# Sorted experts run inside the MLP's block, on two groups of batches, in the MLP's tiles

## The chip, the core and the metric

One core of one Trainium2 chip runs the whole program. The number is the device time of one execution in microseconds, the median of several; a second number is the span of the one execution that the hardware profiler recorded. The engines are PE (TensorE, matmuls and transposes), DVE (VectorE), ACT (ScalarE), POOL (GpSimd) and SP (SyncE, which here only issues DMAs). PEld is PE's weight load, which overlaps its matmuls.

## The reference, cut to what matters

Two layers run one after the other on x of 4 batches x 512 tokens x 256 channels. The first has attention and a 16-expert layer; the second has a gated convolution, an MLP and, last, a top-1 layer of two experts. The change touches only the end of the second layer:

```python
x = x + m                      # the MLP of the second layer, relu(h W_mlp1) W_mlp2, 256 -> 1024 -> 256
h = _layernorm(x) * (1 + cb) + sb
logits = h @ gate_w.T          # 2 experts
probs = softmax(logits)
sel = argmax(probs); top_w = probs[sel]
# each expert: 256 -> 1024 -> 256
y = (silu(h @ w_gate[e].T) * (h @ w_up[e].T)) @ w_down[e].T     # e = sel, for each token
x = x + gb * (top_w * y)       # the output
```

## The kernel before

All arithmetic is fp32, done as products of fp32r pieces: a value is split into a high part (an ACT copy to fp32r) and a low part (a DVE subtraction), and each product is two or three matmuls. B = 4 batches of T = 512 tokens, each TT = 4 tiles of 128 tokens, NT = 16 tiles in all.

**MLP and dispatch** (`mlp_and_dispatch`, one block of five engine programs). `interleave` is the order of every engine: for b in 0 to 5 and i in 0 to 7 it calls `tile(b, i)` (only while b < 4) and the stages written as (back, at, stage), each in turn (b, at) for batch b - back. Turn (b, i) is the name used below. On PE, `up` and `down` are the MLP's matmuls (printed as L49 to L51, the helper `split3`). A batch's dispatch lags its MLP: in turn (b+1, 3) PE transposes the MLP's result to rows (`rows`, L2238) and DVE adds it to X and takes layer-norm statistics (`residual`, L2118, L128); DVE centres and scales the rows (`center_rows` L2134, `scale_rows` L2141) with a root from POOL (L2035); in turn (b+1, 6) PE transposes them back (`columns`, L2247) and ACT and DVE split them into hT (L2072, L2148); in (b+2, 0) PE computes the gate's logits (`gate`, L2259, 16 small matmuls); DVE and ACT turn them into the expert choice and the share (`center`, `exponential` L2081, `choose`); in (b+2, 2) PE counts tokens ahead (`ranks`, L2267, L2268) and DVE writes each token's slot (`place`, L2186); POOL scatters the rows by four indirect DMAs (L2042) into `d_sorted`, expert 0's tokens from the front and expert 1's from the back, over 17 blocks of 128 slots. So turns (4, i) and (5, i) hold only dispatch: that of batch 2 and then the whole chain of batch 3. PS is the PSUM, eight banks: the MLP's tiles use 2 to 5, its result 6 and 7, the dispatch 0 and 1. The second layer's up weights (`up_hi`, `up_lo`) are loaded and split beside the MLP into `u_hi`, `u_lo`.

**Sorted experts** (`sorted_experts`, a block of its own, which begins when every engine has left the block before). SP waits for all scatters, loads blocks of slots into `x_xg` (L2346) and the down weights (L2340). The work is 17 blocks x 4 steps, each of 256 of the 1024 hidden channels. `steps` is the order on each engine: at step s PE does `columns` for the block that starts at s+2 (L2483), `up(s)` (12 matmuls of 512 columns, L2538 to L2540), `rows(s-1)` (two transposes of h, L2506) and `down(s-2)` (L2523 to L2526); ACT does `silu(s)` (L2400) and the high part of h (L2405); DVE does the product (`times`, L2446) and the low part (L2450). Up results alternate over three PSUM banks and transposed h over two. Every block's result goes out by one indirect DMA of POOL to `x_results` (L2375); after the last block all four batches' results are loaded (L2361), multiplied by gb (L2466), added to X (L2470) and stored (L2366). In the first four steps ACT and DVE also split the down weights into `x_w` (L2386, L2422).

Of the kernel before, what the change touches and what calls it, by code (L numbers as in the profile page):

```python
# [15 lines left out]
P = 128  # L16
# [19 lines left out]
L1_BLOCKS = NT + L1_EXPERTS - 1  # L36
# [1861 lines left out]
class Dispatch:  # L1898
# [5 lines left out]
    def __init__(self, k, c):  # L1904
# [3 lines left out]
        self.token, self.back, self.first = sb("token", [NT]), sb("back", [NT]), sb("first", [L1_BLOCKS])  # L1908
# [18 lines left out]
def mlp_and_dispatch(k, conv, H, hT, weights, gate_w, d, up_w, up_d):  # L1927
# [6 lines left out]
    with ExitStack() as c:  # L1934
# [18 lines left out]
        jump = k.sb(n("jump"), [P, TT], F32, c)  # L1953
        S = lambda s: k.sem(n(s))
# [36 lines left out]

        def up_tiles(j):
# [3 lines left out]
        def sync(sp):  # L1996
            def load_rows(b):
# [14 lines left out]
            for i in range(PARTS):  # L2012
# [8 lines left out]
        def gpsimd(pool):  # L2021
            pool.wait_ge(conv.z_ready, B * IT)
# [5 lines left out]
            pool.iota(d.back[:], pattern=[[-P, NT]], base=L1_BLOCKS * P - 1, channel_multiplier=-1,  # L2028
                      allow_small_or_imprecise_dtypes=True).then_inc(filled, 1)
            pool.iota(d.first[:], pattern=[[P, L1_BLOCKS]], base=0, channel_multiplier=0,  # L2030
# [13 lines left out]
            wavefront((0, root), (0, scatter))  # L2044
            yield

        def scalar(act):
            def split(i):
# [38 lines left out]
            yield from interleave(tile, (0, 0, up_part(0, up_hi)), (0, 4, up_part(1, up_hi)), (0, 6, up_part(2, up_hi)), (0, 7, result),  # L2087
                       (1, 0, gate), (1, 6, columns), (2, 1, exponential))

        def vector(dve):  # L2090
            own = Chain(dve, own_dve)
# [21 lines left out]
            def residual(b):  # L2113
# [8 lines left out]
                if b == 0:  # L2122
                    dve.wait_ge(g_hi, 1)
                    dve.tensor_tensor(g2[:, :, 1, :], gst[:], f32(g2[:, :, 0, :]), ALU.subtract).then_inc(g_lo, 1)
                    dve.wait_ge(filled, 4)
# [38 lines left out]
            def choose(b):  # L2164
# [8 lines left out]
                                       initial=d.count[:, b * TT - 1:b * TT] if b else 0.0, op0=ALU.add, op1=ALU.add).then_inc(n_ready, 1)  # L2173
# [5 lines left out]
                own.link(dve.tensor_tensor(jump[:], jump[:], d.token[:, cols], ALU.add))  # L2179
                own.wait()  # L2180

            def place(b):

                cols = slice(b * TT, (b + 1) * TT)
                dve.wait_ge(p_ready, b + 1)
                dve.tensor_tensor(d.slots[:, cols], jump[:], before, ALU.subtract).then_inc(slots_done, 1)  # L2186
                if b == B - 1:
                    dve.wait_ge(t_ready, 1)
                    own.link(dve.tensor_copy(d.n1[:], total))
                    own.wait()  # L2190
                    own.link(dve.tensor_scalar(d.slots_f[:, 0:L1_BLOCKS - 1], d.first[:, 0:L1_BLOCKS - 1], d.n1[:, 0:1], None, ALU.add))
                    own.wait()
                    dve.tensor_scalar(d.expert[:, 0:L1_BLOCKS - 1], d.slots_f[:, 0:L1_BLOCKS - 1], float(B * T), None, ALU.is_ge).then_inc(d.expert_ready, 1)
# [4 lines left out]
            yield from interleave(tile, (0, 1, up_part(0, up_lo)), (0, 5, up_part(1, up_lo)), (0, 7, up_part(2, up_lo)), (0, 7, add_h),  # L2198
                       (1, 3, residual), (1, 4, center_rows), (1, 5, scale_rows), (1, 6, columns_lo), (2, 0, center), (2, 1, choose), (2, 2, place))

        def tensor(pe):
            def up(b, i):
# [434 lines left out]
```

## Time and profile before

| | |
|---|---|
| median of 3 executions | 1180.3 us (1177.23 to 1182.08) |
| the profiled execution: its own time | 1183.18 us |
| its span in the trace | 1181.1 us |
| busy in the span: PE, DVE, ACT, POOL | 81%, 63%, 55%, 39% |
| last large matmul of the MLP begins | 960.92 us |
| last slot of batch 3 written | 981.93 us |
| first expert matmul, last expert matmul | 993.81 us, 1160.22 us |

Times in the trace count from the span's start. A row of a timeline is start, duration, engine, line and operation, and in brackets how long the engine had been idle and what ended that. A row of a table by stretch gives, for each engine, the busy time and the number of instructions, then the clock granted to TensorE (1.00 is 2.4 GHz, 0.50 is 1.2 GHz), then the share of the DMA engines and GB/s.

### The profile page before, as it was taken

What the parts mean: (1) busy time and instruction counts of PE and PEld (TensorE: products, weight loads), DVE (VectorE), ACT (ScalarE), POOL (GpSimd) and SP (SyncE); (2) the same over time, 40 slices, a digit from 0 to 9 for tenths busy, and PEclk for the clock granted to TensorE, in tenths of its full rate; (3) what the DMA queues carried; (4) which work ended last, traced back from release to release, by engine and by line L of the source; (5) the groups of instructions that cost most, each with busy time, mean ns of one, the idle gap of its engine ahead of it and who ended that gap; (6) DMA issues with size and microseconds to landing.
All of it is one profiled execution on the core that took longest, in us unless ns stands there. A gap on an engine that the chain in (4) does not pass through costs nothing. (4 is left out here: it accounts for less than half of the span.)

```text
span 1181.1 us, 21152 instructions
## 1 busy us (share of the span) xinstructions
PE 958.2 (81%) x5454; PEld 800.5 (68%) x5454; DVE 742.6 (63%) x1917; ACT 650.9 (55%) x1693; POOL 454.9 (39%) x637
## 2 busy tenths in 40 slices
PE   6678799999978743678999991479899974999993
PEld 2467688888866632557999990367687753888882
DVE  4875799999956653248655552898546773444444
ACT  3568889999952532248666662469744322333331
POOL 3477466666630665402444443475500221011000
PEclk9788999999988775789999996699899985999996
DMA  6067844444315222309444437410042203001104
GB/s 245 18 211 187 196 104 91 100 91 97 64 50 165 99 77 81 122 25 315 128 127 126 119 109 271 143 72 1 15 128 82 76 28 125 23 28 32 32 15 151
DMA packets 109546, 123.13 MB, mean 104 GB/s; under 512 B 44160, under 2 KB 82560, under 8 KB 109336
## 3 DMA queue, kind: packets, MB, share of 16 engines
q1 hardware_dynamic: 100856, 98.93, 29.4%
q0 software_dynamic: 8608, 23.20, 5.3%
q8 instruction: 40, 0.66, 0.2%
q14 instruction: 42, 0.34, 0.1%
HBM read 77.73 MB, written 44.35 MB: 103 GB/s over the span
## 5 line engine op out<-in xcount | busy, mean ns | idle before, releaser
L741 ACT ACTIVATE PR<-PS,nmax 128x128 f32<-128x128 f32 (+3 forms) x256 | 135.6, 552 | 12.8 <-DVE nmax L781 11.5
L658 POOL TENSOR_SCALAR PR<-PR,rinv 128x128 f32<-128x128 f32 (+3 forms) x256 | 131.9, 536 | 0.0
L781 DVE TENSOR_REDUCE nmax<-PS 128x1 f32<-128x128 f32 (+3 forms) x256 | 113.6, 481 | 19.9 <-PE PS L684 14.3
L1379 POOL DMA_INDIRECT r_results<-r_y,r_to x79 | 75.8, 960 | 113.5 <-DVE r_to L1434 77.3
L789 DVE TENSOR_TENSOR PTlo<-PS,PThi 128x512 fp32r<-128x512 f32 (+1 forms) x192 | 103.0, 590 | 2.9 <-ACT PThi L751 2.9
L751 ACT ACTIVATE PThi<-PS 128x512 fp32r<-128x512 f32 (+1 forms) x192 | 96.8, 545 | 5.7 <-PE PS L696 5.6
L683 PE MATMUL PS<-K,Q 128*128 128x128 f32 (+3 forms) x256 | 84.2, 388 | 10.9 <-DMA Q<-q_parts 6.7
L696 PE MATMUL PS<-ident,PR 128*128 128x128 f32 x640 | 85.8, 279 | 3.2 <-DVE PTlo L789 2.6
L712 PE MATMUL PS<-PThi,V 128*128 128x512 f32 (+3 forms) x256 | 85.3, 346 | 1.0 <-DVE PTlo L789 0.5
L2446 DVE TENSOR_TENSOR x_h<-PS,x_sg 128x256 f32<-128x256 f32 x68 | 28.9, 425 | 86.6 <-ACT x_sg L2400 86.6
L2400 ACT ACTIVATE x_sg<-PS 128x256 f32<-128x256 f32 x68 | 26.2, 385 | 96.0 <-PE PS L2540 96.0
L973 POOL DMA_INDIRECT r_sorted<-o_hrow,o_slots x64 | 64.2, 1004 | 38.5 <-issue 18.7
L2375 POOL DMA_INDIRECT x_results<-x_y,x_to x17 | 16.3, 961 | 157.0 <-DVE x_to L2441 144.6
L712 PE MATMUL PS<-PTlo,V 128*128 128x512 f32 (+3 forms) x256 | 76.2, 323 | 0.0
L1423 DVE TENSOR_TENSOR r_xlo<-PS,r_xhi 128x256 fp32r<-128x256 f32 x79 | 33.4, 423 | 65.8 <-issue 52.5
L696 PEld LDWEIGHTS PS<-ident,PR 128*128 128x128 f32 x640 | 68.7, 142 | 8.8 <-DVE PTlo L789 5.0
L2538 PE MATMUL PS<-r_wlo,r_xhi 128*128 x158 | 59.5, 376 | 2.8 <-issue 2.6
L1394 ACT ACTIVATE r_xhi<-PS 128x256 fp32r<-128x256 f32 x79 | 30.4, 385 | 56.1 <-PE PS L2540 52.7
L683 PEld LDWEIGHTS PS<-K,Q 128*128 128x128 f32 x256 | 51.2, 203 | 13.6 <-issue 6.4
L684 PE MATMUL PS<-maskb,identb 128*128 128x128 bf16 x256 | 60.4, 236 | 0.0
L2524 PE MATMUL PS<-x_w,x_hhi 128*128 (+1 forms) x136 | 57.2, 437 | 1.7 <-DVE x_hlo L2450 1.7
L741 ACT ACTIVATION_READ_ACCUMULATOR PR<-PS,nmax 128x1 f32 x256 | 58.4, 228 | 0.0
(378 smaller groups left out, 3079.6 us busy)
## 6 DMA issues: line engine op xcount, KB each, us to landing
r_xg<-r_sorted SPq DMA_DIRECT2D x79, 129.0 KB
r_wst<-in_routed SPq DMA_DIRECT2D x16, 608.0 KB
K<-k_parts SPq DMA_DIRECT2D x64, 128.0 KB
Q<-q_parts SPq DMA_DIRECT2D x32, 128.0 KB
Q<-q_parts SPq DMA_DIRECT2D x64, 64.0 KB
V<-v_parts SPq DMA_DIRECT2D x64, 64.0 KB, 2.4
mlp_st<-r_results SPq DMA_DIRECT2D x8, 512.0 KB, 7.2
c_yg<-r_results SPq DMA_DIRECT2D x8, 512.0 KB, 8.2
```

The source lines that it names most:

```text
L658: pool.tensor_scalar(PR[:, e % 4, i, 0:w], PR[:, e % 4, i, 0:w], rinv[:, e % 4, i:i + 1], 1.0, ALU.mult, ALU.mult).then_inc(norm_done, 1)
L683: pe.matmul(k.PS[:, i, 0:w], Q4[u][:, s // 2, P * i:P * i + P], K4[u][:, s, 0:w], start=True, stop=False)
L684: pe.matmul(k.PS[:, i, w - P:w], k.identb[:], k.maskb[:], start=False, stop=True).then_inc(s_ready, 1)
L696: ins = pe.transpose(k.PS[:, 4 + bank, at % 512:at % 512 + P], PR[:, (e - TRANS) % 4, i, P * j:P * j + P], k.ident[:])
L712: ins = pe.matmul(O[:, P * j:T], V4[u][:, j, s, :], pt[:, ge % 2, PT_AT[j]:PT_AT[j] + w], start=(s == 0 and j == 0 and part == 0), stop=(s ...
L741: act.activation(PR[:, e % 4, i, 0:w], k.PS[:, i, 0:w], ACT.Exp, bias=nmax[:, e % 4, i:i + 1], accum_out=rsum[:, e % 4, i:i + 1]).then_inc ...
L751: act.activation(PThi[:, e % 2, at:at + w], k.PS[:, 4 + n, 0:w], ACT.Copy).then_inc(hi_done, 1)
L781: dve.tensor_reduce(nmax[:, e % 4, i:i + 1], k.PS[:, i, 0:P * (i + 1)], AX_X, ALU.max, negate=True).then_inc(max_done, 1)
L789: dve.tensor_tensor(PTlo[:, (e - LO) % 2, at:at + w], k.PS[:, 4 + n, 0:w], f32(PThi[:, (e - LO) % 2, at:at + w]), ALU.subtract).then_inc(l ...
L973: pool.indirect_dma_start(out=d.sorted, out_offset=bass.IndirectOffsetOnAxis(ap=slots[:, b * TT + t, choice:choice + 1], axis=0), in_=hrow ...
L1379: pool.indirect_dma_start(out=d.results, out_offset=bass.IndirectOffsetOnAxis(ap=to[:, i % TO_LANES:i % TO_LANES + 1], axis=0), in_=y[:, i ...
L2538: pe.matmul(out, x_hi, w_lo, start=first, stop=False)
```

## The change

`sorted_experts` is no longer a block. It returns programs for each engine, which `interleave` of the renamed `mlp_dispatch_and_experts` advances by one step per turn while b is 4 or 5, ahead of that turn's dispatch stages, and which then run on alone. The tokens are sorted in two groups, batches 0 and 1, and batches 2 and 3, each with 9 blocks (8 + 1 for the boundary between the experts), so there are 18 blocks and 72 steps. A group's blocks need only its own two batches' scatters; the first group's results are loaded beside the second's blocks and added to X in steps 56 to 63; only the second group's follow the last block. The tiles come from those of the MLP: block rows, silu and product in `H`, the down weights in the first two batches of `hT` and in the MLP's weights, others in the MLP's staging. The down weights are split in turns (3, 5), (3, 6) and, the last two, on ACT in (4, 0), (4, 1) and on DVE in (4, 1), (4, 2). PSUM: up results alternate over two banks (before three), transposed h has one (before two).

```diff
+L1_GROUPS = 2
+GROUP_BATCHES = B // L1_GROUPS
+GROUP_BLOCKS = NT // L1_GROUPS + L1_EXPERTS - 1
+L1_BLOCKS = L1_GROUPS * GROUP_BLOCKS
...
-        def interleave(tile, *others):
+        def interleave(experts, tile, *others):
             for b in range(B + 2):
                 for i in range(MLP_T):
                     if b < B:
                         tile(b, i)
+                    else:
+                        next(experts)
                     for back, at, stage in others:
...
+            next(experts)
             load_rows(3)
-            yield
+            yield from experts
...
-            wavefront((0, root), (0, scatter))
+            def first_result(b):
+                if b == B - 1:
+                    next(experts)
+            wavefront((0, root), (0, first_result), (0, scatter))
+            yield from experts
...
-                       (1, 0, gate), (1, 6, columns), (2, 1, exponential))
+                       (1, 0, gate), (1, 6, columns), (2, 1, exponential), (0, 5, down_part(0, x.down_hi(act))), (0, 6, down_part(1, x.down_hi(act))),
+                       (1, 0, down_part(2, x.down_hi(act))), (1, 1, down_part(3, x.down_hi(act))))
...
-        UP, XT, HT, Y = (0, 1, 2), 3, (4, 5), (6, 7)
+    UP, XT, HT, Y = (2, 3), 4, 5, (6, 7)
...
-                wait(pe, h_done, s - 2)
+            wait(pe, h_done, s - 1)
...
-                wait(pe, hlo_done, s - 1)
+            wait(pe, hlo_done, s)
...
+        def load_down(i):
+            if i < 2:
+                sp.wait_ge(own_h, 2 * (i + 1))
+            else:
+                sp.wait_ge(w2_done, i - 1)
...
+        sp.wait_ge(own_h, 6)
+        for i in range(3):
+            load_block(i)
+        load_down(2)
+        load_down(3)
...
+        for i in range(3, N):
+            load_block(i)
+            if i == G + 3:
+                load_results(0)
+        store(0)
+        load_results(1)
+        store(1)
...
+        def first_group(s):
+            at = s - (G + 5) * C
+            if 0 <= at < 4 * GROUP_BATCHES:
+                (added if at % 2 else scaled_rows)(at // 4, at // 2 % 2)
```

How the order moves on PE, after the MLP's last matmul. Before, only dispatch stands there (L2259 gate, L2267 and L2268 ranks, L2238 rows, L2247 columns), then the change of block and the first block's columns (L2483):

```order
L2259 MATMUL PS<-m_g,hT 128x4 x16
L2267 MATMUL PS<-d_count,onesb 128x4
L2268 MATMUL PS<-d_second,later 128x4
L2238 MATMUL PS<-ident,mlp_st 128x128 x8
L2247 MATMUL PS<-ident,m_h 128x128 x8
L2259 MATMUL PS<-m_g,hT 128x4 x16
L2267 MATMUL PS<-d_count,onesb 128x4
L2268 MATMUL PS<-d_second,later 128x4
L2270 MATMUL PS<-d_count,onesb 128x1
L1934 UNCONDITIONAL_BRANCH
L2472 UNCONDITIONAL_BRANCH
L2483 MATMUL PS<-ident,x_xg 128x128 x2
```

Now, from the end of the second expert step's up matmuls in turn (4, 3) (L2629 to L2631 are up, L2583 rows of h, L2289 the dispatch's rows, L2559 columns of a block; `H` and the `m_` tiles are those of the MLP):

```order
L2629 MATMUL PS<-u_lo,m_hi 128x512
L2630 REGISTER_ALU
L2630 MATMUL PS<-u_hi,m_lo 128x512
L2631 MATMUL PS<-u_hi,m_hi 128x512
L2583 MATMUL PS<-ident,H 128x128 x2
L2289 MATMUL PS<-ident,mlp_st 128x128 x8
L2559 MATMUL PS<-ident,H 128x128 x2
L2629 ISA
L2629 MATMUL PS<-u_lo,m_hi 128x512
```

PE's rows for batch 3 now stand behind two expert steps and behind the transposes of h of the first, which wait for ACT and DVE.

On ACT, before, from the MLP's last result (L2062) to the first silu (L2400):

```order
L2062 ACTIVATE mlp_st<-PS,modc 128x512 x2
L2081 ACTIVATE m_ex<-m_lg 128x8
L2072 ACTIVATE hT<-PS 128x512 x2
L2081 ACTIVATE m_ex<-m_lg 128x8
L1934 UNCONDITIONAL_BRANCH
L2380 UNCONDITIONAL_BRANCH
L2395 ACTIVATE x_xhi<-PS 128x256
L2400 ACT_TABLE_LOAD
L2400 ACTIVATE x_sg<-PS 128x256
```

Now, on the same stretch (L2104 the MLP's result, L2467 the block's high part, L2611 the down weights, L2123 the exponential, L2472 silu):

```order
L2104 ACTIVATE mlp_st<-PS,modc 128x512 x2
L2467 ACTIVATE m_hi<-PS 128x256
L2611 ACTIVATE m_whi<-H 128x4x256
L2123 ACTIVATE m_ex<-m_lg 128x8
L2611 ACTIVATE m_wlo<-H 128x4x256
L2472 ACT_TABLE_LOAD
L2472 ACTIVATE H<-PS 128x256 x2
```

Two splits of down weights and a table load now stand between the MLP's last result and the first silu, and batch 3's exponential comes later, between silu(7) and silu(8).


On DVE, in turns (4, 2) to (4, 5), batch 3's residual, statistics, centring and scaling (L2162, L133 to L2165, L2178, L2185) alternate with the experts' product and low part (L2511, L2515):

```order
L2511 TENSOR_TENSOR H<-PS,H 128x256
L2234 TENSOR_TENSOR d_slots<-m_jump,PS 128x4
L2617 TENSOR_TENSOR m_wlo<-H,m_wlo 128x4x256
L2511 TENSOR_TENSOR H<-PS,H 128x256
L2515 TENSOR_TENSOR m_wlo<-PS,m_whi 128x256
L2162 TENSOR_TENSOR X<-PS,X 128x512 x2
L133 BN_STATS m_stats<-X 128x6 x4
L136 BN_AGGR m_mv<-m_stats 128x2 x4
L2165 TENSOR_SCALAR m_var<-m_mv 128x4
L2493 TENSOR_TENSOR m_lo<-PS,m_hi 128x256
L2511 TENSOR_TENSOR H<-PS,H 128x256
```

The third of these rows, a down-weight split, and the product of each step now stand ahead of batch 3's dispatch.

## Rows read from the trace of the kernel before

**Rows 1.** Table by stretch; the columns are explained above.

```profile
961.15:993.81 32.66, 10.92 (x57) 8.87 (x55) 12.21 (x53) 3.84 (x8) 9.02 (x10) 0.55 0.16 52
993.81:1160.62 166.81, 165.05 (x848) 134.75 (x848) 71.09 (x204) 61.29 (x173) 15.37 (x16) 0.98 0.12 39
1160.62:1181.10 20.48, 0.00 (x0) 0.00 (x0) 10.20 (x17) 0.47 (x1) 0.96 (x1) 0.55 0.61 211
1010.97:1143.96 132.99, 132.99 (x702) 109.67 (x700) 55.48 (x169) 47.43 (x140) 13.45 (x14) 1.00 0.08 27
```

**Rows 2.** Timeline: batch 1's last scatter, then from the MLP's end to the experts' start.

```profile
945.51 0.96 POOL L2042 DMA_INDIRECT d_sorted<-m_h,d_slots  x1 [0.30 <-issue]
...
961.15 1.84 PE L2259 MATMUL PS<-m_g,hT 128*128 128x4 f32 x16
...
961.35 1.27 ACT L2062 ACTIVATE mlp_st<-PS,modc 128x512 f32<-128x512 f32 x2 [3.48 <-PE PS L51]
...
986.25 0.96 POOL L2042 DMA_INDIRECT d_sorted<-m_h,d_slots  x1 [0.30 <-issue]
...
992.10 0.69 PE L2483 MATMUL PS<-ident,x_xg 128*128 128x128 f32 x2 [10.41 <-DMA x_xg<-d_sorted]
```

**Rows 3.** Timeline of one steady expert step, engines PE, ACT and DVE.

```profile
1140.71 0.38 PE L2506 MATMUL PS<-ident,x_h 128*128 128x128 f32 x2
...
1141.67 0.41 DVE L2450 TENSOR_TENSOR x_hlo<-PS,x_hhi 128x256 fp32r<-128x256 f32 x1
...
1143.03 0.38 PE L2506 MATMUL PS<-ident,x_h 128*128 128x128 f32 x2
```

**Rows 4.** Groups of instructions, 800 to 1182 us: busy, mean ns, idle before.

```profile
L2446 DVE TENSOR_TENSOR x_h<-PS,x_sg 128x256 f32<-128x256 f32 x68 | 28.9, 425 | 86.6 <-ACT x_sg L2400 86.6
...
L2422 DVE TENSOR_TENSOR x_w<-x_yg,x_w 128x1024 fp32r<-128x1024 f32 x4 | 4.9, 1222 | 1.6 <-ACT x_w L2386 1.6
...
L2386 ACT ACTIVATE x_w<-x_yg 128x1024 fp32r<-128x1024 f32 x4 | 4.2, 1051 | 0.0
```

**Rows 5.** Groups of DVE's instructions, 961 to 993 us.

```profile
L2134 DVE SCALAR_TENSOR_TENSOR m_h<-X,m_mv,mlp_st 128x256 f32<-128x256 f32 x4 | 1.7, 477 | 0.0
...
L128 DVE BATCH_NORM_STATS2 m_stats<-X 128x6 f32<-128x256 f32 x4 | 1.4, 413 | 0.0
...
L2118 DVE TENSOR_TENSOR X<-PS,X 128x512 f32<-128x512 f32 x2 | 1.4, 692 | 1.4 <-PE PS L2238 1.4
```

**Rows 6.** Timeline of the dispatch's transposes at full clock, in turns (3, 3) and (3, 6).

```profile
943.04 1.03 PE L2238 MATMUL PS<-ident,mlp_st 128*128 128x128 f32 x8
...
952.60 1.86 PE L2247 MATMUL PS<-ident,m_h 128*128 128x128 f32 x8 [0.31 <-DVE m_h L2141]
```

**Rows 7.** Timeline of ACT's table load before an exponential.

```profile
909.07 1.28 ACT L2081 ACT_TABLE_LOAD   x1
910.36 0.21 ACT L2081 ACTIVATE m_ex<-m_lg 128x8 f32<-128x8 f32 x1
```

**Rows 8.** Table by stretch, 2 us each, where the clock fell or rose.

```profile
963.00:965.00 2.00, 0.08 (x2) 0.09 (x2) 1.17 (x9) 0.21 (x1) 0.00 (x0) 0.92 0.01 4
965.00:967.00 2.00, 1.44 (x8) 1.38 (x9) 0.66 (x6) 0.00 (x0) 1.04 (x1) 0.50 0.00 0
...
997.00:999.00 2.00, 2.00 (x7) 1.51 (x6) 1.29 (x2) 1.10 (x2) 0.00 (x0) 0.55 0.83 251
999.00:1001.00 2.00, 2.00 (x13) 1.64 (x11) 1.24 (x3) 1.82 (x4) 0.00 (x0) 1.00 1.05 390
```

**Rows 9.** Timeline of the end, from the last result's scatter.

```profile
1162.40 0.96 POOL L2375 DMA_INDIRECT x_results<-x_y,x_to  x1 [4.06 <-DVE x_y L2458]
1164.79 2.02 SPq L2361 DMA_DIRECT2D x_yg<-x_results  x4
1168.65 1.29 DVE L2466 TENSOR_TENSOR x_yg<-x_yg,x_gb 128x512 f32<-128x512 f32 x2 [7.01 <-DMA x_yg<-x_results]
...
1177.09 1.28 DVE L2470 TENSOR_TENSOR X<-X,x_yg 128x512 f32<-128x512 f32 x2
```

More of the change, by code:

```diff
@@ L1924, in __init__, with mlp_dispatch_and_experts @@
         self.done = k.sem("u_done")
-def mlp_and_dispatch(k, conv, H, hT, weights, gate_w, d, up_w, up_d):
+def mlp_dispatch_and_experts(k, conv, H, hT, weights, gate_w, d, up_w, up_d, down_d, out):
     nc = k.nc
@@ L1996, in sync @@
         def sync(sp):
+            experts = x.sync(sp)
             def load_rows(b):
@@ L2268, in ranks @@
                 pe.matmul(before, k.later[:], d.second[:, cols], start=False, stop=True).then_inc(p_ready, 1)
-                if b == B - 1:
-                    pe.matmul(total, k.onesb[:], d.count[:, NT - 1:NT], start=True, stop=True).then_inc(t_ready, 1)
-            yield from interleave(up, (2, 2, ranks), (1, 3, rows), (1, 6, columns), (2, 0, gate),
+                if (b + 1) % GROUP_BATCHES == 0:
+                    pe.matmul(total, k.onesb[:], d.count[:, (b + 1) * TT - 1:(b + 1) * TT], start=True, stop=True).then_inc(t_ready, 1)
+            yield from interleave(experts, up, (2, 2, ranks), (1, 3, rows), (1, 6, columns), (2, 0, gate),
                                   *((0, i + 2, down(i)) for i in range(MLP_T - 2)), (0, 7, down(MLP_T - 2)), (0, 7, down(MLP_T - 1)))
+            yield from experts
         block = c.enter_context(nc.Block())
@@ new lines, in sorted_experts @@
+    G = GROUP_BLOCKS
+    results = k.dram("x_results", [B * T + 2 * P, D])
+    pl = at_places
+    flat = lambda ap: ap.rearrange("p t d -> p (t d)")
+    split_at = lambda ap: ap.rearrange("p e (f a d) -> p e f a d", f=2, a=2)
+    w2, w2st = pl.w2, [flat(ap).rearrange("p (e f d) -> p e f d", e=L1_EXPERTS, f=2) for ap in pl.w2st]
+    xg = flat(pl.xg)[:, 0:3 * ROW].rearrange("p (i e) -> p i e", i=3)
+    two = lambda tile, lane: tile[:, lane, :].rearrange("p (i n) -> p i n", i=2)
+    three = lambda ap: flat(ap)[:, 0:6 * P].rearrange("p (i n) -> p i n", i=3)
@@ new lines, in sorted_experts @@
+    xhi, xlo = two(pl.hi, 0), two(pl.lo, 0)
+    sg, h = (pl.sg[:, 2 * i:2 * i + 2, :] for i in range(2))
+    yr, y = (pl.y[:, 2 * i * D:2 * (i + 1) * D].rearrange("p (i d) -> p i d", i=2) for i in range(2))
+    hhi, hlo = three(pl.hhi), three(pl.hlo)
+    yg, gb = pl.yg, pl.gb.rearrange("p (b d) -> p b d", b=B)
+    spare, share, to, to_done = pl.spare, pl.share, pl.to, k.sem("x_to_done")
+    gb_in = k.sem("x_gb_in")
+    S = lambda s: k.sem("x_" + s)
+    w2_in, w2_hi, w2_done = [S(f"w2_in{i}") for i in range(C)], S("w2_hi"), S("w2_done")
@@ new lines, in load_results, with store @@
+                sp.dma_start(yg[b], rows).then_inc(y_back[b], 16)
+        def store(g):
+            for b in range(g * GROUP_BATCHES, (g + 1) * GROUP_BATCHES):
+                for half in range(2):
+                    sp.wait_ge(x_done, b * 2 + half + 1)
+                    tiles = slice(b * TT + 2 * half, b * TT + 2 * half + 2)
+                    sp.dma_start(out.rearrange("(t p) d -> p t d", p=P)[:, tiles], k.X[:, tiles, :]).then_inc(x_out, 16)
+        load_down(0)
+        load_down(1)
@@ L2531, in moving @@
+    return ExpertPrograms(sync, gpsimd, scalar, vector, tensor, down_hi, down_lo)
 def moving(w, e, cols, depth=P):
```

423 lines of the change are left out of this document (216 added, 207 removed).

## The prediction

> **What bounds the kernel now.** I read the table by stretch first, with the cuts put at the MLP's last matmul and at the experts' first and last [rows 1]. From 993.81 to 1160.62 us PE is busy 165.05 of 166.81 us: the experts' matmuls set the pace. The inner part, 14 blocks from 1010.97 to 1143.96, is 132.99 us with PE never idle and the clock at 1.00: 9.50 us a block, 2.375 us a step. Around it lie two stretches in which PE does little: 32.66 us from 961.15 to 993.81, PE busy 10.92 at a mean clock of 0.55, and 20.48 us after the last matmul. The timeline says what the first of them is [rows 2]: a serial chain through batch 3's dispatch (its last scatter is issued at 986.25), the change of block, the load of the first slots (PE waits 10.41 us, to 992.10) and 1.7 us of splitting the first block. The rows of batches 0 and 1 are sorted long before: their last scatter is issued at 945.51 and, at the 2.4 us that a scatter takes to land at the end (1162.40 to 1164.79 [rows 9]), has landed by 949. The end is one chain too: scatter at 1162.40, results loaded from 1164.79, first multiply at 1168.65, sixteen DVE operations to 1178.37, last store to 1181.1 [rows 9].
>
> **The change, part by part.** The sum is made on the profiled execution's span, 1181.1 us; its own time is 1183.18, 0.2% over the median of 1180.3, so I take the difference of spans off the median.
>
> *The experts start early.* PE's turn (4, 0) is the first block's columns, then batch 2's gate (1.84 us), which ends at about 963.4 after 0.35 us of columns [rows 2]. ACT's MLP results end at 962.62 [rows 2], then high part and low part of the block cost 0.4 us each, about 963.5. So up(0) starts at 963.6 instead of 993.81. The block rows are there (scatters over at 949, SP's three loads follow). Down weights 0 and 1 are split in turns (3, 5) to (3, 7) by 1.05 us on ACT and 1.22 us on DVE each [rows 4], in gaps in which both wait for PE now; covered.
>
> *One block more:* 18 x 9.50 = 171.0 us where 17 were 161.5. That is +9.5 us on the path, with no cover.
>
> *The dispatch's own matmuls* now lie between expert steps. At full clock batch 3 costs 1.03 us for rows and 1.86 for columns [rows 6], 1.84 for the gate and 0.3 for ranks: 5.0 us on PE.
>
> *Waits in the shared turns.* Engines are in order, so I walk the queues with the durations of the rows. The first silu stands on ACT behind down split 3. Its load is issued only when DVE has finished split 1, at about 962.2, lands some 4 us later (the loads of results took 3.86 from issue to first use [rows 9]), so the split ends at 967.4, the table load at 968.6 (1.28 [rows 7]), silu(0) at 969.0 and the product at 969.5. PE has done up(0), ranks and up(1) by 966.7 and stands at the transposes of h: 2.9 us idle. Behind it are batch 3's rows, and behind these DVE's residual (two of 0.69), statistics (1.4, with their aggregation 1.8), centring and scaling (1.7 each) [rows 5]. DVE has one product and one low part (0.42 each [rows 4]) between each of them; PE waits for the product of each step. This gives columns of batch 3 at 980.9, the gate at 987.3 to 989.1, the exponential with a table load there and one back (2 x 1.28), slots of batch 3 at 995, and up(9) at 994.1. Nine steps without anything would end at 963.6 + 21.4 = 985.0; the excess of 9.1 is the 5.0 of PE work and 4.1 of waits. Bounds of the waits: 2 us, if only the first silu's wait is paid, and 12, if batch 3's DVE work (residual to splitting hT, 8 us, and 2 us of choosing) is paid in full by PE.
>
> *The clock.* It is at 0.50 about 3.7 us after the MLP's last large matmul, while PE did only the small gate matmuls and waited, and comes back between 997 and 999, some 4 us after up matmuls had begun [rows 8]. In the new order the same gate is followed by 2.8 us of up matmuls and then by the 2.9 us wait, so I expect a fall at about 970 and a return after 4 to 6 us of dense work. A step's PE work of 2.375 us then takes twice that; half of this hides in the waits for DVE. Cost 3 us, bounds 0 and 6.
>
> The Trainium skill (TensorE: Matmul & The Clock Gate, "HAM oscillation") says that gaps between bursts of matmuls can make every burst start at half clock. If this held for all ten shared turns they would cost their doubled PE work, 24 us more less the waits. Rows 8 show the clock back within the first steps of dense up matmuls, and here PE has such a step in each turn, so I price one fall.
>
> *Sum to PE's end.* up(9) at 994.1 + 3 = 997.1; 63 steps x 2.375 = 149.6; drain 2.4 (now: 1010.97 is step 6, 62 more steps end at 1158.2, the last matmul at 1160.62). PE ends at 1149.1, now 1160.62: -11.5.
>
> *Single buffers.* rows(s) must now wait for the low part of h of step s-1. In the steady step the transposes stand at 1140.71 and 1143.03 and the low part between them ends at 1142.08 [rows 3]: 0.95 us to spare. The second up bank is free earlier than that. The first group's eight DVE operations of 0.69 us (steps 56 to 63) fit in DVE's idle time, of 132.99 us it works 55.48 [rows 1]. Cost nothing; if the cover goes, each 0.1 us a step is 7 us.
>
> *Scatter, loads.* POOL puts the first result ahead of batch 3's scatter, in turn (5, 0), before the slots exist: nothing. The second group's blocks are needed at step 36, about 1061, and are scattered by 1002. SP's wait for the first group's results holds back loads needed ten steps later.
>
> *The end.* Eight DVE operations instead of sixteen. Now sixteen take 9.7 us (1168.65 to 1178.37 [rows 9]), two independent ones after each other; the new order alternates multiply and dependent add, which shows their full length, 0.69 (L2118, of the same size [rows 5]) and a hand-over: 8 x 0.71 = 5.7. The first result is still 8.0 us after PE's end, the last store 2.7. 8.0 + 5.7 + 2.7 = 16.4 against 20.48: -4.0; bounds -2.5 (second load late) and -5.
>
> Sum: -11.5 - 4.0 = -15.5; 1180.3 - 15.5 = 1164.8, rounded 1165 us.
>
> One more rule bears on the silu and exponential that now alternate. The trace's table load is 1.28 us and the exponential follows it at once, at 910.36 [rows 7]. The Trainium skill (ScalarE: Activation LUTs, "What ACT_TABLE_LOAD costs") gives 1283 ns and about 1380 ns of drain, 2.66 us a switch; three switches would be 4 us more on ACT, and as an estimate from that page the sum would be 1168. The row shows the first part and no drain, so I leave it out.
>
> **The rivals.**
>
> *Little is lost in the shared turns* (0.22). The clock does not fall, because up(0) and up(1) come in time, or the waits are half: 3 + 2 us less, 1159 to 1161. For it: up(0) and up(1) are 2.8 us of large matmuls inside that stretch. Against it: gate, ranks and transposes keep PE on small work for most of 961 to 971.
>
> *The shared turns are expensive* (0.20). PE goes to ACT and DVE and back in every step, at half clock until the gate of batch 3 is past; waits are 10 instead of 4 and the clock costs 6: 1170 to 1174. For it: each shared turn holds up to 1.8 us more for DVE, which stands between PE's steps. Against it: PE queues up(s+1) ahead of rows(s), so that a delay of one product is covered by 1.4 us.
>
> *No early start* (0.06). Something in the first steps waits until batch 3 is dispatched, a DMA that SP issues too late, as SP now waits for two scatters and for DVE's splits between loads. Then the 32.66 us stay save for the change of block and the slots' load (about 8), one block of 9.5 is added, the end gives 4: 1178, no change.
>
> *Slower* (0.06): the steady pace drops because of the one PSUM bank for transposed h. The chain transposes, ACT copy, DVE low part, transposes would have to take over 2.32 us a step; it is 1.37 now. If it lost 0.3 us in each of 72 steps, 21.6 us, the time would be 1186; it decides from 0.2 us a step. Rows 3 speak against it.
>
> **How the numbers follow.** The forecast, 1161 to 1170, has 0.46; the rivals as given. The likeliest case gives 1165. The range reaches over the cheap and the expensive shared turns, 1157 to 1174, and leaves out 0.12 for the last two and something for the unforeseen. A measurement of this kernel tells 0.5%, 6 us, from no change. Faster than 1174: the first three cases, less a part of the expensive one, 0.86; same 0.08; slower 0.06.
>
> **What the new profile would show.** First up matmul (L2629) near 964, not 994. PE idle before the first transposes of h by about 3 us, released by DVE's product, and ACT's silu behind a down split that waited for a DMA. The clock at 0.50 once, somewhere in 968 to 977. Batch 3's last slot near 998. Then 9.50 us a block to about 1149, with no PE idle and no wait at L2583. Eight DVE operations at the end, and a stretch of 16 to 17 us after PE's last matmul. A block time over 9.6 us, a first up matmul after 975, or a clock at half for more than 10 us would make the prediction wrong.

## The result and the profile after

The changed kernel takes 1157.13 us (median of 4 executions, 1156.89 to 1159.51), beside 1180.28 us (1177.23 to 1182.08) for the kernel before: ratio 0.9822, interval 0.9802 to 0.9842. The forecast was 1165, range 1157 to 1174. The profiled execution has a span of 1155.7 us (before 1181.1). In it the expert stages are L2559 (a block's columns), L2629 to L2631 (up), L2583 (rows of h), L2599 to L2602 (down); those of the dispatch on PE are L2310, L2318, L2289, L2298.

The table by stretch, with the cuts of [rows 1]: MLP's end, first up matmul, PE's last matmul, end; and below, 14 steady blocks from step 10's columns on. Columns as there.

```profile
955.43:957.76 2.33, 2.06 (x19) 1.97 (x18) 1.61 (x4) 2.13 (x4) 0.00 (x0) 1.00 0.05 17
957.76:1139.70 181.94, 177.59 (x935) 146.42 (x935) 88.50 (x273) 67.42 (x187) 25.97 (x26) 0.98 0.15 47
1139.70:1155.70 16.00, 0.00 (x1) 0.00 (x0) 5.75 (x9) 0.47 (x1) 0.96 (x1) 0.63 0.42 139
990.24:1122.80 132.56, 132.56 (x702) 109.79 (x701) 60.20 (x177) 47.62 (x140) 16.63 (x18) 1.00 0.15 47
```

The 32.66 us between MLP and experts are 2.33 us now. The steady blocks cost 132.56 / 14 = 9.47 us each (before 9.50 [rows 1]), with PE never idle. The stretch after PE's last matmul is 16.0 us, not 20.48.

A difference of spans of 25.4 us is more than the change gives. The MLP ends at 955.43 here and at 961.15 before [rows 2], though from the transposes of turn (3, 3) to there it takes 18.1 us in both; in another execution of this same kernel it ends at 961.50. So the 5.7 us are variation between executions, and I count from the MLP's end: 219.95 us before, 200.27 in this execution, 201.4 and 200.1 in the two controls below. **The change is worth 18.6 to 19.9 us**, counted against one execution of the kernel before, and the ratio of medians says 21 with ±2.4.

The timeline of the start (start, duration, engine, line, operation, and the idle time before with what ended it):

```profile
955.29 1.23 DVE L2617 TENSOR_TENSOR hT<-H,hT 128x1024 fp32r<-128x1024 f32 x1
955.43 0.38 PE L2559 MATMUL PS<-ident,H 128*128 128x128 f32 x2
...
957.76 0.49 PE L2629 MATMUL PS<-u_lo,m_hi 128*128 x1 [0.28 <-DVE m_lo L2493]
...
961.25 1.06 ACT L2611 ACTIVATE m_wlo<-H 128x1024 fp32r<-128x1024 f32 x1 [2.91 <-DMA H<-in_down]
962.33 1.28 ACT L2472 ACT_TABLE_LOAD   x1
963.62 0.66 ACT L2472 ACTIVATE H<-PS 128x256 f32<-128x256 f32 x2
...
964.52 0.69 PE L2583 MATMUL PS<-ident,H 128*128 128x128 f32 x2 [3.58 <-DVE H L2511]
```

This is the chain that was foreseen: DVE's split 1 is over at 956.5, only then may the last down weights be loaded, ACT waits 2.91 us for them with the fourth split, then loads its table, and the first silu comes at 963.62. PE stands 3.58 us at the first transposes of h. The table of PE's waits from 955 to 1140 us (total, times, longest) has nothing else of size:

```profile
PE PS L2583 <- DVE H L2511: 3.6, 1, 3.6
PE PS L2583 <- DVE m_wlo L2515: 0.4, 1, 0.4
```

The clock, in a table by stretch of 2 us each:

```profile
961.00:963.00 2.00, 0.00 (x0) 0.00 (x0) 0.00 (x0) 1.73 (x2) 0.00 (x0) 1.00 0.47 164
963.00:965.00 2.00, 0.48 (x2) 0.48 (x3) 0.96 (x3) 1.27 (x3) 0.18 (x1) 0.52 0.00 0
965.00:967.00 2.00, 2.00 (x12) 2.00 (x11) 1.97 (x5) 0.39 (x1) 1.69 (x2) 0.50 0.00 0
967.00:969.00 2.00, 2.00 (x7) 1.61 (x6) 1.97 (x5) 0.38 (x1) 1.70 (x2) 0.50 0.37 132
969.00:971.00 2.00, 2.00 (x11) 1.57 (x10) 1.60 (x9) 0.67 (x2) 1.67 (x3) 0.77 0.22 81
```

In this execution it falls while PE is idle, at about 963, stays at 0.50 (1.2 GHz) for the first transposes of h, batch 3's rows and one step's up matmuls, and is back at about 970. Between 970 and the end of PE's work it does not fall again.

And the end, where eight DVE operations stand instead of sixteen:

```profile
1139.31 0.39 PE L2600 MATMUL PS<-m_wlo,m_whi 128*128 128x512 f32 x1
...
1141.49 0.96 POOL L2453 DMA_INDIRECT x_results<-mlp_st,x_to  x1 [4.45 <-DVE mlp_st L2523]
1143.95 0.37 SPq L2422 DMA_DIRECT2D mlp_st<-x_results  x1
...
1147.67 0.69 DVE L2529 TENSOR_TENSOR mlp_st<-mlp_st 128x512 f32<-128x512 f32 x1 [6.95 <-DMA mlp_st<-x_results]
...
1152.38 0.69 DVE L2534 TENSOR_TENSOR X<-X,H 128x512 f32<-128x512 f32 x1
```

The first operation starts 7.97 us after PE's end and the last ends at 1153.07, 2.6 us before the end: 8.0 + 5.4 + 2.6.

### The profile page after: what moved, and what is told of

Read it like the earlier page. It is cut to its first block and busy times, and to the rows that moved or that the text cites. A ratio compares the mean times of both kernels' runs of the same rounds, so it can differ in the third digit from the quotient of the medians.

```text
span 1155.7 us, 21305 instructions
## 1 busy us (share of the span) xinstructions
PE 957.4 (83%) x5505; PEld 801.8 (69%) x5505; DVE 746.7 (65%) x1932; ACT 657.2 (57%) x1705; POOL 458.8 (40%) x641
## 5 line engine op out<-in xcount | busy, mean ns | idle before, releaser
L2511 DVE TENSOR_TENSOR H<-PS,H 128x256 f32<-128x256 f32 x72 | 30.6, 424 | 81.9 <-ACT H L2472 80.2
L2472 ACT ACTIVATE H<-PS 128x256 f32<-128x256 f32 x72 | 27.6, 385 | 97.2 <-PE PS L2631 96.1
L2453 POOL DMA_INDIRECT x_results<-mlp_st,x_to x18 | 17.4, 966 | 143.0 <-DVE x_to L2506 118.7
L2629 PE MATMUL PS<-r_wlo,r_xhi 128*128 x158 | 59.1, 374 | 2.5 <-issue 2.4
L2629 PE MATMUL PS<-u_lo,m_hi 128*128 (+1 forms) x144 | 59.1, 411 | 0.3 <-DVE m_lo L2493 0.3
```

The costliest lines, as they stand in the source:

```text
L2629: pe.matmul(out, x_hi, w_lo, start=first, stop=False)
```

## The experiments

Totals of two kernels cannot be told apart here under some 4 us, so each run is read in the trace at marks that do not depend on what came before: the dispatch's transposes of batch 2 (L2289, turn (3, 3)), the MLP's end (the first block's columns), step 6's columns (turn (4, 6)), PE's end. The kernel called the control is the changed kernel, unaltered.

**Control.**

> The changed kernel again, unaltered, on the chip of the three runs beside it. 1157 us. In its trace: first up matmul 2.3 us after the first block's columns (955.43 to 957.76 before), one wait of about 3.6 us at the first transposes of h, PE's last matmul about 184 us after those columns, 16.0 us behind it.

Measured: 1159.59 us, ratio 0.9827 (0.9811 to 0.9844), span 1162.9. From the MLP's end to step 6's columns 23.10 us (961.50 to 984.60), in the first execution 23.11; to the end 201.4, because PE lost 1.06 us once at 1003.74, where ACT had stood still for a reason that the trace doesn't show; the first execution did not.

This stop of ACT comes back at the same place, between the columns of steps 10 and 14, in most of the runs below. PE's wait for it is nothing in the first execution, in the second control and with the late addition, 0.3 to 0.4 us in the second early splits and the splits in the gap, and 1.1 to 1.4 us with more banks, the first early splits, the late split, both, and the clock fill. Since one kernel shows it in one execution and not in another, no edit is needed for it; a comparison that runs to the end contains it, and one that stops at step 6 doesn't. The rows are those of the clock fill:

```profile
1002.60 0.38 ACT L2472 ACTIVATE H<-PS 128x256 f32<-128x256 f32 x1 [3.65 <-PE PS L2634]
...
1003.92 0.41 PE L2586 MATMUL PS<-ident,H 128*128 128x128 f32 x2 [1.40 <-DVE m_wlo L2515]
```

**What one group does: 17 blocks, no early start.**

```diff
-L1_GROUPS = 2
+L1_GROUPS = 1
...
-                    else:
-                        next(experts)
```

with results loaded and added only at the end, as in the kernel before; tiles, PSUM banks, the common block and the early down weights stay as changed.

> One group of 17 blocks that needs all four batches, no overlap, still in the MLP's block and tiles, all results added at the end. Against the kernel with two groups and no overlap: one block less (-9.5 us), the first loads behind the last scatter (+9.6: scatters 5 us of issue, 2.4 to land, 2 to load), sixteen DVE operations at the end (+4.1). Theory: 1175 us, some 5 us under the kernel before, which is what the merged block and the early split of the down weights are worth. Rival, that the block change itself is dear: 1165 us or less.

Measured: 1177.83 us, ratio 0.9984 (0.9966 to 1.0002). PE's first block columns come 31.3 us after the MLP's end (957.72):

```profile
961.54 1.23 DVE L2609 TENSOR_TENSOR m_whi<-H,m_whi 128x1024 fp32r<-128x1024 f32 x1
...
984.19 0.96 POOL L2076 DMA_INDIRECT d_sorted<-m_h,d_slots  x1 [0.30 <-issue]
...
986.95 1.28 SPq L2409 DMA_DIRECT2D H<-d_sorted  x3
...
989.04 0.69 PE L2551 MATMUL PS<-ident,H 128*128 128x128 f32 x2 [9.47 <-DMA H<-d_sorted]
```

Before, they came after 30.95 us with a wait of 10.41 [rows 2], and the load of the slots stood here:

```profile
989.94 1.27 SPq L2346 DMA_DIRECT2D x_xg<-d_sorted  x3
```

What the columns wait for in both is the load of the slots, behind batch 3's last scatter. The two halves of this path differ, though. From the last scatter's start to the load it is 2.76 us, where it was 3.69, and to the columns 4.85 where it was 5.85: **the change of block had cost 1.0 us**. From the MLP's end to that scatter it is 26.47 us, where it was 25.10: 1.4 us more, since two of DVE's splits of down weights now stand in the chain, one ahead of batch 2's slots (the row of 961.54, the slots at 962.68) and one ahead of batch 3's residual. From the columns to step 6's columns it is 16.36 us where it was 18.87: 2.5 us less, of which 1.7 are two waits of PE for DVE's low part that stood behind the splits of down weights before and are gone. The stretch after PE's end is 21.6 us, 1.1 more than before: sixteen operations in the alternating order, as the prediction said of that order. Together these give 1 us, which the time can't tell from nothing.

**Two groups, but no turn shared with the dispatch.** `next(experts)` is taken out of `interleave` (the last two lines of the diff above, alone).

> The experts' programs are not advanced in the turns of b = 4 and 5; they start when the dispatch of batch 3 is through. Everything else (two groups, 18 blocks, tiles, one block of programs, the early addition of the first group) stays. Theory, that the gain is the overlap: dispatch chain 20.4 us as in the kernel before, first up matmul 22.5 us after the MLP's end, half clock for its first 4 us (2.5 us lost): about +14 us against the control, 1171 us. Rival, that the gain comes from leaving out the change of block and the first loads behind it, and the overlap is paid back by stalls: under +4 us, 1157 to 1161 us.

Measured: 1172.57 us, ratio 0.9937 (0.992 to 0.9953), 13.0 us over the control. The first columns come 22.7 us after the MLP's end (959.62 to 982.35, no wait for a load), step 6's after 38.35:

```profile
982.35 0.67 PE L2557 MATMUL PS<-ident,H 128*128 128x128 f32 x2
...
997.97 0.38 PE L2557 MATMUL PS<-ident,H 128*128 128x128 f32 x2
```

At step 6 the shared turns are 38.35 - 23.10 = 15.2 us ahead, but the rest of batch 3's dispatch is then still to come between the control's steps. The pace of the later blocks is the control's, 9.46 us. To the end it is 213.3 against 201.4, **12 us, by medians 13**, and 13 against the two executions without ACT's stop. Against one group (31.3 to the first columns) the start is 8.6 us earlier, because no scatter and no load of batch 3's rows stands ahead of it.

**The first group's results added only at the end.**

```diff
-            if i == G + 3:
-                load_results(0)
-        store(0)
+        load_results(0)
         load_results(1)
+        store(0)
...
-        for b in range(GROUP_BATCHES, B):
+        for b in range(B):
```

> The changed kernel, but the first group's results are loaded, scaled, added and stored only behind the last block, as all results are in the kernel before. Theory: eight DVE operations come back at the end, 0.69 to 0.71 us each where they alternate: +5 us, the stretch behind PE's last matmul 21 instead of 16 us, 1162 us. Rival, that the loads set the end: +1 us or less, since both groups' loads run side by side.

Measured: 1159.11 us, ratio 0.9824 (0.9808 to 0.9841), against the control's 1159.59. I expected 5 us more; there is no difference. The timeline of DVE says why: the first group's results are in long before, and their eight operations run while DVE waits for the second group's anyway.

```profile
1142.83 0.68 DVE L2528 TENSOR_TENSOR H<-H,mlp_st 128x512 f32<-128x512 f32 x1
...
1147.53 0.69 DVE L2533 TENSOR_TENSOR X<-X,H 128x512 f32<-128x512 f32 x1
1150.51 0.69 DVE L2528 TENSOR_TENSOR mlp_st<-mlp_st 128x512 f32<-128x512 f32 x1 [2.29 <-DMA mlp_st<-x_results]
```

The stretch after PE's end (1141.88) is 16.6 us, 0.6 over the first execution's: POOL's scatter takes 1.40 us beside DVE's work instead of 0.96, and the load comes as much later. It doesn't show in the time; in this execution step 6 came after 21.9 us, 1.2 sooner than in the control (the clock, below). So of the 4.5 us that the end is shorter, some 3.9 come from the grouping of the results' loads, and 0.6 from the adding in steps 56 to 63.

**The clock.** Fifteen matmuls of 512 columns, whose result is never read, stand ahead of the first transposes of h, where PE is idle in the control. They fill 3.5 us.

```diff
         def rows(s):
+            if s == 0:
+                for _ in range(15):
+                    pe.matmul(k.PS[:, HT, :], xhi[:, 0, 0:P], up_w.hi[:, 0, 0:4 * P], start=True, stop=True)
```

> The changed kernel with 15 added matmuls of 512 columns (0.23 us each at full clock) ahead of PE's first transposes of h, into a bank that these transposes overwrite; they add work of 3.5 us where PE idles 3.6 us and change no result. Theory, that the clock falls because of the idle time and costs about 2 us: it stays at 1.00, step 6's columns at 21 to 22 us. Rival, that the fall is due to the small gate matmuls before, or costs nothing because DVE is late anyway: step 6's columns still at 23 us or later.

Measured: 1165.13 us, ratio 0.9842 (0.9811 to 0.9873). The clock never falls:

```profile
969.00:971.00 2.00, 2.00 (x10) 1.50 (x8) 0.10 (x1) 1.97 (x4) 0.00 (x0) 1.00 0.08 28
```

Step 6's columns come after 22.14 us, 0.96 before the control's. **The fall of the clock costs 1.0 us up to there, not 3.** Full speed runs into DVE: at the third transposes of h PE waits 0.98 us for the low part, which in the control, at half clock, it doesn't.

```profile
977.62 0.41 PE L2586 MATMUL PS<-ident,H 128*128 128x128 f32 x2 [0.98 <-DVE m_wlo L2515]
```

To the end nothing of the 1.0 us is left in this execution, since ACT's stop takes 1.40 us in it (the table below).

The run with the late addition shows that the price depends on where the fall lies. There the clock fell 3.8 us after the MLP's end, where it was 7.7 in the control: on the up matmuls of step 1 and not in the wait, and was back while PE stood waiting for the first product:

```profile
963.00:965.00 2.00, 2.00 (x5) 1.56 (x6) 1.07 (x1) 0.55 (x1) 0.00 (x0) 0.50 0.90 308
965.00:967.00 2.00, 0.67 (x2) 0.00 (x0) 0.00 (x0) 1.97 (x3) 0.00 (x0) 0.72 0.15 52
```

Its first wait is 2.05 us instead of 3.5, and step 6's columns come after 21.88 us, no later than with the fill: this fall cost nothing. The instructions up to there are the control's.

**More banks.** From step 24 on three PSUM banks hold up results and two transposed h, as before the change (the dispatch's two are free by then).

```diff
-    UP, XT, HT, Y = (2, 3), 4, 5, (6, 7)
+    XT, Y = 4, (6, 7)
+    S0 = 24
+    UPB = lambda s: (2, 3)[s % 2] if s < S0 else (2, 3, 0)[(s - S0) % 3]
+    HTB = lambda s: 5 if s < S0 else (5, 1)[(s - S0) % 2]
```

> The changed kernel, but from step 24 on, when the dispatch has left its two PSUM banks, up results alternate over three banks and transposed h over two, as in the kernel before. Theory, that the single buffers cost nothing: the pace of the later blocks stays at 9.47 us and the time at the control's, within 1 us. Rival, that they cost a hidden bit per step: 48 steps at 0.05 us would be 2.4 us.

Measured: 1165.6 us, ratio 0.9835 (0.9802 to 0.9868). Between the columns of two late blocks:

```profile
1124.17 0.38 PE L2562 MATMUL PS<-ident,H 128*128 128x128 f32 x2
...
1133.63 0.38 PE L2562 MATMUL PS<-ident,H 128*128 128x128 f32 x2
```

9.46 us, and in the control 9.46 too (1120.52 to 1129.98). The single banks cost nothing in the steady steps. In the last two steps, where no up matmuls stand between, PE waits 0.4 and 0.2 us in the control and not here; from the last block's columns to PE's end that makes 16.6 us instead of 17.0.

**Where the down weights are split.** In these the first silu's wait was to be shortened. Numbers in brackets are turns.

```diff
 late split:   ACT split 3 (4, 1) -> (4, 2), DVE split 3 (4, 2) -> (4, 3)
 early splits: ACT splits 0, 1 (3, 5), (3, 6) -> (3, 3), (3, 4); DVE (3, 6), (3, 7) -> (3, 4), (3, 5)
 both:         both of these
```

> The changed kernel with the last split of down weights one turn later, on ACT behind silu(0) and on DVE in turn (4, 3), so that the first silu no longer waits for that load. Counted from the first block's columns, step 6's columns were at 23.1 us in the changed kernel and its control. Theory, that the 3.6 us wait is due to this load alone: the wait shrinks to 1 us or less, the clock does not fall or falls later, step 6's columns at 18.5 to 19.5 us, the time 4 us under the control. Rival, that DVE's work for batch 3 is next in line and takes over: 0 to 1 us gained, with PE waiting for a later product instead.

> The changed kernel with the first two splits two turns earlier (ACT in (3, 3) and (3, 4), DVE in (3, 4) and (3, 5)), so that the loads of the last two are issued some 5 us earlier. Theory: the split that silu(0) waits for finds its load landed, silu(0) 2.9 us earlier, step 6's columns at 19 to 20.5 us; but DVE has 2.4 us more in the turns in which it is most busy in the MLP, which may cost PE up to 2 us there. 2 to 4 us under the control. Rival: the loss in the MLP eats the gain, no difference.

> The first two pairs of down splits stand two shared turns earlier, over six rounds this time beside the control. Theory (the cluster around the third and fourth down split is what holds up the first silu): step 6's columns 19 to 20.5 us after the first block's, 3 to 4 us earlier than the control, of which 0.9 us is lost again in the MLP's last turns, where DVE's m_h comes late; the time 2 to 3 us under the control, 0.2 to 0.3%. Rival (what is won at the start is given back before the end, by waits at the third rows or a lower pace): no difference from the control, though step 6 comes earlier.

> The first two pairs of down splits two shared turns earlier, and the fourth pair one turn later, so that the first silu stands behind no split that waits for a load. Theory (both delays are separate): step 6's columns 18.5 to 19.5 us after the first block's, the first rows with a wait under 1 us, the time 3 to 4 us under the control. Rival (the rows that need down_lo wait instead, as they did with the late split alone, 3 waits of 3.4 us together): step 6's columns at 19 to 20.5 as with the early splits alone, and the time the same as that run's.

Measured, in us. The late split, the first early splits and the clock fill ran beside a kernel before of 1184.97 us, the control, the second early splits and both beside 1178.19, the last (below) beside 1178.96, so between these sets only the ratios compare.

| | to MLP's end from L2289 (3, 3) | MLP's end to step 6 | sum | from L2289 (3, 3) to the end | of it ACT's stop | time | ratio |
|---|---|---|---|---|---|---|---|
| control, again | 18.07 | 23.02 | 41.09 | 218.2 | 0 | 1161.43 | 0.9841 (0.981 to 0.9871) |
| late split | 18.07 | 20.52 | 38.59 | 217.2 | 1.4 | 1165.42 | 0.9848 (0.9816 to 0.9881) |
| early splits | 20.51 | 19.15 | 39.66 | 218.1 | 1.1 | 1164.11 | 0.9832 (0.9802 to 0.9863) |
| early splits, again | 20.49 | 19.15 | 39.64 | 217.2 | 0.3 | 1159.93 | 0.9832 (0.98 to 0.9863) |
| both | 20.51 | 19.29 | 39.80 | 218.3 | 1.3 | 1158.14 | 0.983 (0.9801 to 0.9859) |
| clock fill | 18.06 | 22.14 | 40.20 | 218.9 | 1.4 | 1165.13 | 0.9842 (0.9811 to 0.9873) |
| splits in the gap | 18.08 | 19.17 | 37.25 | 214.9 | 0.4 | 1156.6 | 0.9814 (0.9793 to 0.9834) |

The ratios' intervals all overlap, so no order among these kernels is shown by their times. From step 6 to the end they lose little but ACT's stop: without it each gain up to step 6 is a gain to the end too, within 0.3 us.

The late split takes the wait for the product away. DVE's split then stands ahead of the third step's product and low part, and PE waits for that:

```profile
971.64 0.41 PE L2583 MATMUL PS<-ident,H 128*128 128x128 f32 x2 [1.59 <-DVE m_wlo L2515]
```

(Of the 3.4 us in three waits that the expectation of the run with both splits names, 1.4 are ACT's stop and 0.4 the wait of PE's last steps, which the control has too.) It wins 2.5 us of the 4 expected up to step 6; the clock fell 4 us earlier here, as with the late addition, so that what of the 2.5 us is the split's is not separated. The early splits win 3.9 us at the start and give 2.4 back in the MLP, where I had counted 0.9. The timeline of their second run and, below it, the table by stretch show both halves of the loss: DVE's first split (948.01) pushes back the rows' scaling, PE waits 1.16 us for it instead of 0.31, and this idleness and the eight short transposes are followed by half clock, which doubles the MLP's matmuls for some 3 us.

```profile
948.01 1.22 DVE L2617 TENSOR_TENSOR hT<-H,hT 128x1024 fp32r<-128x1024 f32 x1
...
951.50 2.19 PE L2298 MATMUL PS<-ident,m_h 128*128 128x128 f32 x8 [1.16 <-DVE m_h L2185]
```

```profile
949.00:951.00 2.00, 1.34 (x6) 0.76 (x5) 2.00 (x4) 0.60 (x1) 0.00 (x0) 1.00 0.30 71
951.00:953.00 2.00, 1.36 (x6) 0.82 (x7) 2.00 (x5) 0.04 (x1) 0.00 (x0) 0.97 0.57 197
953.00:955.00 2.00, 2.00 (x8) 1.71 (x7) 2.00 (x4) 1.16 (x2) 0.00 (x0) 0.50 0.07 25
955.00:957.00 2.00, 2.00 (x7) 1.60 (x7) 0.47 (x1) 0.00 (x0) 0.00 (x0) 0.67 0.79 222
```

Both together win no more than the early splits alone (the rival of that run): PE waits 1.60 us for the low part, as with the late split, where the early splits alone have waits of 0.55 and 1.00 us for the product. What is left is DVE's own work.

**Splits in the gap.** This is what the two halves suggest: DVE's first two splits behind the rows' scaling, in the 0.45 us gap before the split of hT that nobody waits for soon, and ahead of the MLP's last additions (1.2 us each), which in the control keep split 1, and with it the last load, until then.

```diff
-  (0, 5, down_part(0, x.down_hi(act))), (0, 6, down_part(1, x.down_hi(act))),
+  (0, 5, down_part(0, x.down_hi(act))), (0, 5, down_part(1, x.down_hi(act))),
...
-  (1, 5, scale_rows), (1, 6, columns_lo), (2, 0, center), (2, 1, choose), (2, 2, place),
-  (0, 6, down_part(0, x.down_lo(dve))), (0, 7, down_part(1, x.down_lo(dve))), ...
+  (1, 5, scale_rows), (0, 6, down_part(0, x.down_lo(dve))), (0, 6, down_part(1, x.down_lo(dve))),
+  (1, 6, columns_lo), (2, 0, center), (2, 1, choose), (2, 2, place), ...
```

> DVE's first two down splits stand in turn (3, 6), right behind the scaling of batch 2's rows and ahead of the split of hT, and ACT's first two both in turn (3, 5); so DVE's centring and scaling are not pushed back, and the second split is done before the MLP's last additions instead of behind them. Theory (the early splits gained 3.9 us at the start and gave 2.4 back in the MLP, by a late m_h and half a clock): from the transposes of rows in turn (3, 3) to the first block's columns 18.1 us as in the control (20.5 with the early splits), PE's wait there 0.3; from those columns to step 6's 19 to 20 us (control 23.0), so the two together 37 to 38 us against 41.1 in the control and 39.6 with the early splits; the time 3 to 4 us under the control, a ratio to the kernel before near 0.981. Rival (the split of hT, now 2.4 us later, or the MLP's last turn, pays instead): 20 us or more to the first block's columns and 39 to 41 together.

Measured: 1156.6 us (5 executions), ratio 0.9814 (0.9793 to 0.9834).

```profile
947.53 1.86 PE L2298 MATMUL PS<-ident,m_h 128*128 128x128 f32 x8 [0.32 <-DVE m_h L2185]
949.09 2.35 DVE L2617 TENSOR_TENSOR hT<-H,hT 128x1024 fp32r<-128x1024 f32 x2
950.34 1.94 SPq L2406 DMA_DIRECT2D H<-in_down  x4
...
958.98 1.04 ACT L2611 ACTIVATE m_wlo<-H 128x1024 fp32r<-128x1024 f32 x1
960.04 1.28 ACT L2472 ACT_TABLE_LOAD   x1
961.33 0.76 ACT L2472 ACTIVATE H<-PS 128x256 f32<-128x256 f32 x2
...
962.23 0.44 PE L2583 MATMUL PS<-ident,H 128*128 128x128 f32 x2 [0.55 <-DVE H L2511]
```

Both splits are over at 951.4 and all loads are issued by 952.3. ACT's fourth split waits for nothing, PE's first wait is 0.55 us, and the clock stays at 1.00 through the MLP's end and the shared turns. From L2289 to step 6 it is 37.25 us, 3.8 under the control, inside what was expected. From the MLP's end to the end it is 196.8 us (the executions of the changed kernel without ACT's stop 200.1 and 200.3, before 219.95): 3.3 us under them. It has the lowest ratio of all; its interval overlaps the control's, so that it is faster is shown by the trace of one execution and not by its time.

## Why the prediction was right, and where its sum was off

The direction, the mechanism and the range held. From the MLP's end the prediction's numbers give 204.4 us to the end (span 1165.6 less 961.15); 200.3 were measured in the first execution, 201.4 and 200.1 in the controls. Step by step, from the MLP's end in the first execution:

| | predicted | measured |
|---|---|---|
| up(0) | +2.45 | +2.33 |
| up(9) | +35.95 | +32.13 |
| PE's end, from up(9) | 152.0 | 152.1 |
| after PE's end | 16.4 | 16.0 |

- **The start at once**: right, and the run without shared turns shows that it is worth 12 to 13 us.
- **The dispatch's own matmuls**, 5.0 us: too much. The row of 1.86 us for the columns [rows 6] was taken as PE's cost, but it includes the waiting between the transposes, as DVE's four scaled tiles come one after the other. From start to next start they take 0.79 us in turn (4, 5) (975.36 to 976.15), the gate 1.70, the ranks 0.1, and the rows 0.88 where they ran at full clock (late addition, 967.99 to 968.87): 3.5 us.
- **Waits**, 4.1 us, of them 2.9 for the first silu: 3.6 from up(0) to up(9), all of it the first one, at the cause that was named (the product came 0.7 us later than reckoned). Of the 1.2 us for DVE's pace nothing appeared: the 0.4 us of the table stands at PE's last steps. It was not that DVE has room: in the five runs whose clock was full in these turns (fill, late addition, both early splits, splits in the gap) it makes PE wait 1.0 us at the third transposes of h. Half clock and DVE's lateness cover each other, and I had added them.
- **The clock**, 3 us: the fall happened once, around the first wait, as said, was over after 7 us, and cost 1.0 us up to step 6; in two other executions it came 4 us earlier, and in one of these it cost nothing. The step that failed is the price of work at half clock, which fell on transposes and up(2) that DVE held up anyway. With these three the excess of nine steps is 3.5 + 3.6 + 1.0 = 8.1 us, where 12.1 stood in the sum (5.0 + 4.1 + 3); 8.5 were measured.
- The Trainium skill (TensorE: Matmul & The Clock Gate, "HAM oscillation") says that gaps between bursts of matmuls can make every burst start at half clock, which the forecast priced at up to 24 us. The rows of the clock show one fall in ten shared turns; in the other turns of the first execution PE has no wait over 0.3 us, so the case that the page describes hardly arises here.
- **The table loads.** The exponential between two silus costs its two loads and nothing beside:

```profile
985.10 1.28 ACT L2123 ACT_TABLE_LOAD   x1
986.40 0.21 ACT L2123 ACTIVATE m_ex<-m_lg 128x8 f32<-128x8 f32 x1
986.62 1.28 ACT L2472 ACT_TABLE_LOAD   x1
...
987.92 0.39 ACT L2472 ACTIVATE H<-PS 128x256 f32<-128x256 f32 x1
```

  The drain of about 1380 ns that the Trainium skill (ScalarE: Activation LUTs, "What ACT_TABLE_LOAD costs") adds is not in these rows: each instruction starts 0.01 to 0.02 us after the one before it. PE did not wait here. (With that drain three times the forecast's sum would have come to 1169, not to the 1168 that it states.)
- **One block more**, +9.5: right, 9.47 a block. **Single banks**, 0: right in the steady steps, 0.4 us at PE's end, by the run with more banks. **Scatter and loads**, 0: right.
- **The end**, -4.0: -4.5 measured, the right size for the wrong reason, which is luck. I counted eight operations fewer because they run in steps 56 to 63. The late addition shows that they are free at the end too. What makes the end shorter is that half the results no longer wait for the last block, so that DVE can deal with them before the others arrive.

An account, each term from one run against another: no wait for batch 3's scatter and load -8.3 (30.95 to 22.7; the change of block, 1.0, and the splits in the dispatch's chain, 1.4 the other way, are in it), one block more +9.5, the end -4.5, a shorter way from the first columns to step 6 -2.5, shared turns -12 to -13: -17.8 to -18.8, where 18.6 to 19.9 were measured. Some 1 us stays open. The forecast was 8 us over the measured median. The sum above makes 4.1 us of that; the rest lies ahead of the MLP's end, which the profiled execution reached 5.7 us earlier than that of the kernel before.

## What to carry to other kernels

Splitting work into groups pays one block for its edge (9.5 us here), and a start that waits for fewer loads won hardly that back (8.3 us); it pays through what it makes possible, a first group that runs in the idle turns of another chain (12 to 13 us) and a tail that handles half its data during a wait (3.9 us). A load may stand behind a cheap operation that was placed late on a busy engine: what released the last load here was a 1.2 us DVE split behind the MLP's additions, and moving it into a gap where nobody waited won 3.8 us up to step 6 and 3.3 to the end, while moving it two turns earlier, ahead of work that PE did wait for, gave most of the gain back. When waits and half clock fall in the same turns, their prices are not to be added.

## What the runs showed of the hardware

- The clock fell without a long stall: in the second early splits PE was busy for 1.34 and 1.36 us of two stretches of 2 us, with a wait of 1.16 us and eight transposes in them, and was then at 0.50 for about 3 us; in the changed kernel, idle for 0.45 us at that place, it stayed at 1.00. A delay of 0.85 us became a loss of 2.4 us.
- One program did not show the fall at one place: 7.7 us after the first block's columns in the control, PE being idle, and 3.8 us after them with the late addition and the late split, PE being busy between the up matmuls of two steps.
- It was back at about 970 in the first execution, after transposes and one step's up matmuls at 0.50, and at about 966 with the late addition, while PE stood idle.
- The transposes' row in a timeline can hold their waiting: 1.86 us against 0.79 from start to start for the same eight.
- POOL's indirect DMA instruction takes 0.96 us in most rows, beside DVE's statistics and operations that read PSUM too. It took longer beside DVE's TENSOR_TENSOR operations on SBUF alone: 1.21 us (no shared turn), 1.40 (one group) and 1.76 (changed kernel) beside a split of down weights, 1.40 beside the additions at the end of the late addition.
- ACT stood still for some 1 to 2.4 us at one place of its program in eight of eleven executions, with its inputs there; no run shows why.
- The same instructions ahead of the MLP's end took from 955.4 to 964.9 us in executions of one kernel and of kernels that differ from it only behind that point.
